# A segment sum and two-layer MLP on one NeuronCore: TensorE's step 0 written out in front of its loop

## The chip, the cores and the metric

The kernel runs on one core of a Trainium2 chip. The metric is the device time of one execution in microseconds (us), the median over several runs. TensorE (PE) does the matmuls, VectorE (DVE), ScalarE (ACT) and GpSimd (POOL) the rest, and SyncE (SP) issues the large DMAs. Each engine works through its own list of instructions, and the engines meet at semaphores.

## The reference

412,500 edges, each with 48 features and a destination node, sorted by destination; 12,500 nodes with 128 features.

```python
h   = maximum(layernorm(x), 0)                     # nodes x 128
agg = segment_sum(edge_attr_48, dst, 12500)        # nodes x 48
u   = graph_globals[0]                             # 64, the same for all nodes
z   = relu(concat([h, agg, u]) @ W1 + b1)          # 240 -> 256
out = x + z @ W2 + b2                              # 256 -> 128
```

## The kernel before

**Tiling.** The edges are cut into groups of 896 (128 partitions with 7 edges each). 19 groups are one step, and there are 25 steps, the last a short one. The nodes are cut into 25 tiles of 512. A step's groups come in five quads: quads 0 to 2 are part 0 (12 groups), quads 3 and 4 are part 1 (7 groups). The edge buffer holds one step; SP loads a quad of the next step when TensorE signals (`edges_used`) that it has used that quad of this one.

**Sums.** For each quad VectorE writes a onehot matrix (`make_onehot`, L795): which of 32 nodes following the group's first an edge belongs to. TensorE multiplies it with the edges into `group_bank` (`sum_quad`, L1043; a 32-column tile for each group). ScalarE copies a part's sums to SBUF (`copy_sums`), VectorE makes the rest of the split (`low_sums`, L831), and TensorE places the part's windows at their nodes with a second onehot matrix, `placing` (`place`, L1065). VectorE adds the placed window to `agg` (`add_window`, L824).

**Positions.** `placing` needs to know where each group stands in its window. GpSimd works that out for all steps at once at the start (`places`, which ends with `spread`, L468). TensorE turns it with five transposes (`turn_places`, L1116) and VectorE copies the result to `const_bank` (L891), after which it can write the first `placing` (L807). VectorE takes its work in the order of the program: behind that copy stand the first `placing`, the moments of the first node tile, more onehots, the `low_sums` of part 1 and the `agg` adds.

**MLP.** `turn_x(k)` (L1082) transposes the normalised node tile k; `first_layer(k)` (L1092, L1096, L1098) and `second_layer(k)` (L1109) run one and two steps after it.

**TensorE's program.** After a few matmuls that keep its clock up (`keep_clock`, L1131) and the transposes of the first destinations (`turn_rel`, L1028), TensorE runs a hardware loop over steps 0 to 23, one body for all of them, with branches for what differs: L1145 (`i > blocks`; `blocks` is 4), L1148 (`i > 1`), L1152 (`i > 0`) and L1159 (`i > 0` around the first layer). In step 0 it takes the branches to `turn_places`, the last block in the chain of Else parts, and past the first layer. In step 1 it takes those to `sum_bias` (L1124). Behind the loop stand the short last step and the end of the MLP.
Of the kernel before, what the change touches and what calls it, by code (L numbers as in the profile page):

```python
# [60 lines left out]
def gnn_kernel(nc, x, dst, edges, graph_globals, w1, b1, w2, b2, out):  # L61
# [8 lines left out]
    full_steps = n_edges // step_edges  # L70
# [22 lines left out]
    with ctx:  # L93
# [6 lines left out]
        def sem(name):  # L100
            return ctx.enter_context(nc.semaphore(name))
# [96 lines left out]
        rel_ready = sem("rel_ready")  # L198
# [57 lines left out]
        def quads_of(s):  # L256
            return LAST_QUADS if s.static and s.value == steps - 1 else QUADS

        def part_quads(s, h):
            if s.static and s.value == steps - 1:  # L260
                return PART_QUADS[0][:len(LAST_QUADS)] if h == 0 else ()
            return PART_QUADS[h]
# [9 lines left out]
        def strips_of(k):  # L272
            return last_width // P if k.value_is_last else NJ
# [6 lines left out]
        def own(k):  # L280
            return 1 if k.static and k.value == tiles - 2 else 0
# [741 lines left out]
        def _(pe):  # L1023
# [9 lines left out]
            def sum_quad(s, q):  # L1033
                g0, ng = quads_of(s)[q]
                h = 0 if q in PART_QUADS[0] else 1
                n = q - PART_QUADS[h][0]
                pe.wait_ge(edges_in[q], s.value * 16 + 16)
                pe.wait_ge(onehot_ready, s.value * NQ + q + 1)
                if n == 0:
                    pe.wait_ge(sums_split[h], s.value + 1)  # L1040
                for r in range(EDGES_PER_ROW):
                    for j in range(ng):
                        done = pe.matmul(  # L1043
                            group_bank[h][WINDOW * j:WINDOW * (j + 1), n * F_EDGE:(n + 1) * F_EDGE],
                            onehot[:, (g0 + j) * EDGES_PER_ROW + r, :],
                            edge_buf[:, g0 + j, r * F_EDGE:(r + 1) * F_EDGE],
                            start=(r == 0), stop=(r == EDGES_PER_ROW - 1))
                done.then_inc(edges_used, 1)

            def sum_part(s, h):  # L1050
                for q in part_quads(s, h):
                    sum_quad(s, q)

            def place(s, h):
                quads = part_quads(s, h)
                pe.wait_ge(sums_split[h], s.value + 2)
                pe.wait_ge(placing_ready[h], s.value + 1)
                if not s.below(1):
                    pe.wait_ge(agg_added, s.value * 2 + h + 2)
                bank = window_bank[h][0:F_EDGE, :].rearrange("f (j i) -> f j i", j=NJ)  # L1060
                for n, q in enumerate(quads):
                    low, high = QUAD_WINDOW[q]
                    rows = quads_of(s)[q][1] * WINDOW
                    for part, sums in enumerate((sums_high, sums_low)):
                        done = pe.matmul(bank[:, :, low // NJ:high // NJ], sums[h][0:rows, n, :],  # L1065
                                         placing[h][0:rows, n, :, 0:(high - low) // NJ],
                                         start=(n + part == 0), stop=(n == len(quads) - 1 and part == 1),
                                         skip_group_check=True)
                done.then_inc(window_ready[h], 1)

            def turn_x(k, to_bank=turned_bank):
                pe.wait_ge(normed, k.value + 1)
                if to_bank is not turned_bank:
                    pe.wait_ge(sums_split[1], full_steps + 1)
                elif isinstance(k, Again):
                    pe.wait_ge(out_copied, k.value + 2)
                else:
                    pe.wait_ge(position_ready, 1)
                    pe.wait_ge(out_copied, k.value + 1)
                pe.wait_ge(turned_copied, k.value + 1)  # L1080
                for j in range(strips_of(k)):
                    done = pe.transpose(to_bank[:, j * P:(j + 1) * P], normed_x[:, j, :], ident[:, :])  # L1082
                done.then_inc(x_turned, 1)

            def first_layer(k):
                pe.wait_ge(w1_split, 1)
                pe.wait_ge(bias_ready, 3)
                pe.wait_ge(turned_copied, k.value + 2)
                cols = strips_of(k) * P
                for c in range(2):  # L1090
                    pe.wait_ge(hidden_copied, k.value * 2 + c + 5)
                    pe.matmul(hidden_bank[c][:, 0:cols], w1_node[:, c * P:(c + 1) * P], normed_t[own(k)][:, 0:cols],  # L1092
                              start=True, stop=False)
                pe.wait_ge(tile_low_ready, k.value + 3)
                for c in range(2):
                    pe.matmul(hidden_bank[c][:, 0:cols], w1_high[:, c * P:(c + 1) * P], tile_sums[own(k)][:, 0:cols],  # L1096
                              start=False, stop=False)
                    pe.matmul(hidden_bank[c][:, 0:cols], w1_low[:, c * P:(c + 1) * P], tile_sums[own(k)][:, 0:cols],  # L1098
                              start=False, stop=True).then_inc(hidden_ready, 1)

            def second_layer(k, to_bank=out_bank):
                pe.wait_ge(hidden_copied, k.value * 2 + 8)
                if to_bank is out_bank:
                    pe.wait_ge(out_copied, k.value + 2)
                    if not isinstance(k, Again):
                        pe.wait_ge(turned_copied, k.plus(2).value + 1)
                for j in range(strips_of(k)):
                    for c in range(2):
                        done = pe.matmul(to_bank[:, j * P:(j + 1) * P], hidden[own(k)][:, c, j * P:(j + 1) * P],  # L1109
                                         w2_sb[:, c, :], start=(c == 0), stop=(c == 1))  # L1110
                done.then_inc(out_ready, 1)

            def turn_places():
                pe.wait_ge(spread_ready, 1)
                for q in range(NQ):
                    done = pe.transpose(out_bank[:, q * steps:(q + 1) * steps],  # L1116
                                        spread[:, q, :, :].rearrange("s j w -> s (j w)"), ident[0:steps, 0:steps])
                done.then_inc(position_turned, 1)

            def sum_bias():  # L1120
                pe.wait_ge(weights_in, 7 * 16)
                pe.wait_ge(rel_ready, 2)
                for c in range(2):
                    done = pe.matmul(hidden_bank[c][:, 0:1], w1_global[:, c * P:(c + 1) * P], global_col[:, :],  # L1124
                                     start=True, stop=True)
                done.then_inc(bias_summed, 1)

            def keep_clock(n, bank):
                ones16 = ones[:, :].bitcast(mybir.dt.bfloat16)
                with pe.Fori(0, n):  # L1130
                    pe.matmul(bank[:, 0:2 * P], ones16[:, 0:P], ones16[:, :], start=True, stop=True)  # L1131
# [7 lines left out]
            keep_clock(8, window_bank[0])  # L1139
            turn_rel(0)  # L1140
            keep_clock(4, window_bank[0])
            with pe.Fori(0, full_steps) as i:
                step = At(0, i)
                sum_part(step, 0)
                with pe.If(i > blocks):  # L1145
                    second_layer(step.plus(-2))
                with pe.Else():
                    with pe.If(i > 1):  # L1148
                        second_layer(step.plus(-2))
                        turn_rel(i - 1)  # L1150
                    with pe.Else():
                        with pe.If(i > 0):  # L1152
                            sum_bias()
                        with pe.Else():
                            turn_places()
                place(step, 0)
                sum_part(step, 1)
                turn_x(step)
                with pe.If(i > 0):  # L1159
                    pe.wait_ge(rel_ready, i * 2)  # L1160
                    first_layer(step.plus(-1))
                place(step, 1)

            final, third, second, last = At(steps - 1), At(tiles - 3), At(tiles - 2), last_tile()
# [63 lines left out]
```

## Time and profile before

| | us |
|---|---|
| median of 3 runs | 270.75 (270.53 to 270.99) |
| the profiled execution | 270.22 |
| its span | 268.1 |
| TensorE busy | 244.8 (91%) |
| VectorE busy | 228.2 (85%) |
| ScalarE / GpSimd busy | 144.3 / 104.2 |
| bytes moved | 94.48 MB, 352 GB/s over the span |
| mean granted TensorE clock | 0.968 of full |

The span is the time between the first and the last instruction of the trace; the profiled execution's time is 2.1 us longer. A granted clock of 1.00 is 2.4 GHz and 0.50 is 1.2 GHz.

### The profile page before, as it was taken

The page shows a single profiled execution, that of the slowest core. Times are in us where ns is not written, and L with a number is a line of the kernel's source. Part 1 is how long each engine was busy: PE and PEld are TensorE (multiplying, and loading weights), DVE is VectorE, ACT ScalarE, POOL GpSimd, SP SyncE. Part 2 cuts the span into 40 slices and gives each one's busy share as a digit, 9 for nine tenths or more (in the row PEclk, how much of TensorE's full clock was granted, in tenths as well). Part 3 has the DMA queues.
Part 4 walks back from the last instruction along what each step waited for, and adds up shares of the span by engine and source line. Part 5 has one row for each costly group of instructions (what it writes and reads, how often), then busy time and mean ns, then how long its engine had stood idle before and what let it go on. Part 6 is the DMA issues. An engine that isn't in the chain of part 4 may idle for free.

```text
span 268.1 us, 17351 instructions
## 1 busy us (share of the span) xinstructions
PE 244.8 (91%) x7438; PEld 199.4 (74%) x7438; DVE 228.2 (85%) x556; ACT 144.3 (54%) x315; POOL 104.2 (39%) x112
## 2 busy tenths in 40 slices
PE   6647699999999999989899989999999989999994
PEld 3546678878878977877787777786797777778753
DVE  1967977898899999988999899999999999897362
ACT  2904447867654755455465366465365545546541
POOL 8761031351453255235135325415424514523410
PEclk9965789999999999999999999999999999999999
DMA  7999989999999999999999999999999999999941
GB/s 246 366 362 349 353 273 333 340 371 328 334 378 380 388 382 381 373 380 381 388 381 382 389 382 382 370 366 374 384 369 367 385 381 383 386 373 317 397 185 55
DMA packets 70873, 94.48 MB, mean 352 GB/s; under 512 B 4324, under 2 KB 64260, under 8 KB 70854
## 3 DMA queue, kind: packets, MB, share of 16 engines
q1 hardware_dynamic: 69802, 94.29, 99.6%
q10 hardware_dynamic: 956, 0.00, 0.2%
q14 instruction: 15, 0.12, 0.1%
q8 instruction: 4, 0.07, 0.1%
q0 software_dynamic: 96, 0.00, 0.0%
HBM read 87.88 MB, written 6.40 MB: 352 GB/s over the span
## 4 chain that ended last, share of the span: by engine, by line
PE 55%; DMA 25%; DVE 12%; issue 5%; DVEq 1%; POOL 1%; ACT 0%; POOLq 0%
DMA edge_buf<-in_edge_attr 23%; PE group_bank L1043 19%; PE out_bank L1109 11%; PE hidden_bank L1092 10%; DVE onehot L795 4%; PE window_bank L1065 4%; PE out_bank L1082 3%; PE hidden_bank L1096 3%; PE hidden_bank L1098 3%; PE hidden_bank L1028 2%; DMA dst_rows<-in_dst 1%; DVE placing L807 1%; DVE bn L840 1%; DVE agg L824 1%; DVE rel_rows L750 1%
## 5 line engine op out<-in xcount | busy, mean ns | idle before, releaser
L795 DVE TENSOR_TENSOR onehot<-rel,const_bank 128x896 f32<-128x896 f32 (+1 forms) x122 | 122.8, 1023 | 8.0 <-issue 7.9
L1043 PE MATMUL group_bank<-edge_buf,onehot 128*32 128x48 f32 x6454 | 89.2, 212 | 5.0 <-DMA edge_buf<-in_edge_attr 3.6
L1043 PEld LDWEIGHTS group_bank<-edge_buf,onehot 128*32 128x32 f32 x6454 | 81.3, 114 | 11.5 <-issue 7.0
L536 POOL TENSOR_TENSOR tile_sums<-agg,tile_sums 48x512 fp32r<-48x512 f32 x23 | 29.2, 1268 | 137.8 <-ACT tile_sums L623 137.8
L1109 PE MATMUL out_bank<-w_sb,hidden 128*128 128x128 f32 x384 | 48.5, 279 | 1.7 <-issue 0.9
L1109 PEld LDWEIGHTS out_bank<-w_sb,hidden 128*128 128x128 f32 x384 | 44.7, 191 | 4.1 <-issue 1.3
L1092 PE MATMUL hidden_bank<-normed_t,w_node 128*128 128x512 f32 (+1 forms) x100 | 46.9, 591 | 0.4 <-ACT hidden L633 0.4
L601 ACT ACTIVATE normed_x<-x_buf,shift,inverse 128x128 f32<-128x128 f32 x98 | 40.3, 492 | 1.3 <-DVE shift L855 1.3
L633 ACT ACTIVATE hidden<-hidden_bank,hidden_bias 128x512 f32<-128x512 f32 (+1 forms) x50 | 31.3, 676 | 11.5 <-PE hidden_bank L1098 11.5
L593 ACT ACTIVATE deviation<-mean_var,eps_col 128x4 f32<-128x4 f32 (+1 forms) x25 | 7.5, 298 | 52.0 <-DVE mean_var L846 52.0
L519 POOL TENSOR_TENSOR xb_buf<-x_buf,b_rows 128x512 f32<-128x512 f32 (+1 forms) x25 | 31.5, 1262 | 7.5 <-DMA x_buf<-in_x 4.2
L531 POOL TENSOR_TENSOR out_buf<-mlp_out,xb_buf 128x512 f32<-128x512 f32 x23 | 29.4, 1277 | 5.6 <-ACT mlp_out L641 3.9
L824 DVE TENSOR_TENSOR agg<-agg,window_bank 48x352 f32 (+1 forms) x49 | 21.6, 441 | 10.7 <-PE window_bank L1065 9.8
L641 ACT ACTIVATE mlp_out<-out_bank 128x512 f32<-128x512 f32 x23 | 13.7, 597 | 29.4 <-PE out_bank L1109 29.4
L1096 PE MATMUL hidden_bank<-tile_sums,w_high 112*128 112x512 f32 (+1 forms) x50 | 29.1, 582 | 0.1
L1065 PE MATMUL window_bank<-placing,sums_high 128*48 128x128 f32 (+3 forms) x122 | 23.1, 247 | 5.6 <-DVE sums_low L831 4.2
L1092 PEld LDWEIGHTS hidden_bank<-normed_t,w_node 128*128 128x128 f32 x100 | 17.3, 194 | 12.8 <-issue 12.6
L807 DVE TENSOR_TENSOR placing<-node_ramp,const_bank 128x456 fp32r<-128x456 f32 (+2 forms) x49 | 24.9, 508 | 0.0
L623 ACT ACTIVATE tile_sums<-agg 48x512 fp32r<-48x512 f32 (+1 forms) x25 | 15.6, 625 | 14.5 <-DVE agg L824 12.1
L1065 PE MATMUL window_bank<-placing,sums_low 128*48 128x128 f32 (+3 forms) x122 | 21.5, 232 | 0.0
L1065 PEld LDWEIGHTS window_bank<-placing,sums_high 128*48 128x48 f32 (+1 forms) x122 | 15.2, 126 | 8.2 <-issue 7.1
L840 DVE BATCH_NORM_STATS2 bn<-x_buf 128x6 f32<-128x128 f32 x98 | 21.0, 271 | 0.0
(97 smaller groups left out, 219.5 us busy)
## 6 DMA issues: line engine op xcount, KB each, us to landing
edge_buf<-in_edge_attr SPq DMA_DIRECT2D x97, 672.0 KB, 7.0
edge_buf<-in_edge_attr SPq DMA_DIRECT2D x24, 504.0 KB, 7.7
x_buf<-in_x SPq DMA_DIRECT2D x24, 256.0 KB, 7.9
out<-out_buf SPq DMA_DIRECT2D x23, 256.0 KB, 5.8
dst_rows<-in_dst SPq DMA_DIRECT2D x3, 448.5 KB, 6.3
dst_rows<-in_dst SPq DMA_DIRECT2D x1, 252.3 KB
out<-out_buf SPq DMA_DIRECT2D x1, 224.0 KB
edge_buf<-in_edge_attr SPq DMA_DIRECT2D x1, 168.0 KB, 5.4
```

Of the source, the lines that this page charges most:

```text
L519: pool.tensor_tensor(xb_buf[k.third][:, 0:nj, :], x_buf[k.parity][:, 0:nj, :], b2_rows[:, :].unsqueeze(1).to_broadcast([P, nj, F_NODE]), A ...
L531: pool.tensor_tensor(out_buf[slot(k)][:, 0:nj, :], mlp_out[:, 0:nj, :], xb_buf[k.third][:, 0:nj, :], ALU.add).then_inc(out_added, 1)
L536: pool.tensor_tensor(sums_tile(k, STACK_LOW), agg_tile(k), sums_tile(k, 0).bitcast(fp32), ALU.subtract)\
L601: done = act.activation(normed_x[:, j, :], x_buf[k.parity][:, j, :], ACT.Relu, bias=shift[:, j:j + 1], scale=inverse[:, j:j + 1])
L633: act.activation(hidden[own(k)][:, c, 0:cols], hidden_bank[c][:, 0:cols], ACT.Relu, bias=hidden_bias[:, c:c + 1]).then_inc(hidden_copied, 1)
L795: dve.tensor_tensor(onehot[:, c0:c0 + cols, :], rel[:, r0:r0 + cols].unsqueeze(2).to_broadcast([P, cols, WINDOW]), ramp_const.unsqueeze(1) ...
L807: dve.tensor_tensor(placing[h][:, 0:nq, :, 0:width], node_ramp[:, :, 0:width].unsqueeze(1).to_broadcast([P, nq, NJ, width]), position_cons ...
L1043: done = pe.matmul(group_bank[h][WINDOW * j:WINDOW * (j + 1), n * F_EDGE:(n + 1) * F_EDGE], onehot[:, (g0 + j) * EDGES_PER_ROW + r, :], ed ...
L1065: done = pe.matmul(bank[:, :, low // NJ:high // NJ], sums[h][0:rows, n, :], placing[h][0:rows, n, :, 0:(high - low) // NJ], start=(n + par ...
L1092: pe.matmul(hidden_bank[c][:, 0:cols], w1_node[:, c * P:(c + 1) * P], normed_t[own(k)][:, 0:cols], start=True, stop=False)
L1096: pe.matmul(hidden_bank[c][:, 0:cols], w1_high[:, c * P:(c + 1) * P], tile_sums[own(k)][:, 0:cols], start=False, stop=False)
L1109: done = pe.matmul(to_bank[:, j * P:(j + 1) * P], hidden[own(k)][:, c, j * P:(j + 1) * P], w2_sb[:, c, :], start=(c == 0), stop=(c == 1))
```

## The change

TensorE's step 0 stands in front of the loop, in the order in which the loop's body did it: the sums of part 0, `turn_places`, the placing of part 0, the sums of part 1, `turn_x`, the placing of part 1. Its waits are on constants. The loop runs from step 1, without the branch of L1152 and without that of L1159. No other engine's program changes. The static program of TensorE becomes longer by one step's instructions and shorter by two branches; the matmuls that run, and their order, stay the same.

```diff
             keep_clock(4, window_bank[0])
-            with pe.Fori(0, full_steps) as i:
+            sum_part(At(0), 0)
+            turn_places()
+            place(At(0), 0)
+            sum_part(At(0), 1)
+            turn_x(At(0))
+            place(At(0), 1)
+            with pe.Fori(1, full_steps) as i:
                 step = At(0, i)
                 sum_part(step, 0)
                 with pe.If(i > blocks):
@@
                         second_layer(step.plus(-2))
                         turn_rel(i - 1)
                     with pe.Else():
-                        with pe.If(i > 0):
-                            sum_bias()
-                        with pe.Else():
-                            turn_places()
+                        sum_bias()
                 place(step, 0)
                 sum_part(step, 1)
                 turn_x(step)
-                with pe.If(i > 0):
-                    pe.wait_ge(rel_ready, i * 2)
-                    first_layer(step.plus(-1))
+                pe.wait_ge(rel_ready, i * 2)
+                first_layer(step.plus(-1))
                 place(step, 1)
```

## Rows read from the trace of the kernel before

**Rows 1.** The page: its header, and the chain's shares by engine

```profile
span 268.1 us, 17351 instructions
...
PE 55%; DMA 25%; DVE 12%; issue 5%; DVEq 1%; POOL 1%; ACT 0%; POOLq 0%
```

**Rows 2.** The chain that ended last, 0 to 45 us: start, us, what

```profile
12.70 1.26 POOL spread L468
13.96 1.86 issue
...
16.59 0.31 DVE const_bank L891
...
30.93 0.23 DVE sums_low L831
```

**Rows 3.** TensorE in order of time: start, us, what [idle before <-releaser]

```profile
9.19 3.21 PE L1043 MATMUL group_bank<-edge_buf,onehot 128*32 128x48 f32 x168 [1.37 <-DVE onehot L795]
15.82 0.72 PE L1116 MATMUL out_bank<-ident,spread 25*128 25x25 f32 x5 [3.42 <-issue]
17.79 0.34 PE L1065 MATMUL window_bank<-placing,sums_high 128*48 128x128 f32 x1 [1.24 <-DVE placing L807]
...
18.66 2.46 PE L1043 MATMUL group_bank<-edge_buf,onehot 128*32 128x48 f32 x98
22.06 1.11 PE L1082 MATMUL out_bank<-ident,normed_x 128*128 128x128 f32 x4 [0.94 <-ACT normed_x L601]
...
24.53 3.59 PE L1043 MATMUL group_bank<-edge_buf,onehot 128*32 128x48 f32 x168
28.29 0.87 PE L1124 MATMUL hidden_bank<-global_col,w_global 64*128 64x1 f32 x4 [0.17 <-issue]
31.29 0.26 PE L1065 MATMUL window_bank<-placing,sums_high 128*48 128x128 f32 x1 [2.12 <-DVE sums_low L831]
```

**Rows 4.** Branch instructions by line: count, ns min/median/max, first and last start

```profile
L1148 PEldq COMPARE_BRANCH  x1: 3099/3099/3099, 12.4 to 12.4; - x1
```

```profile
L1159 PEldq COMPARE_BRANCH  x1: 439/439/439, 22.1 to 22.1; - x1
```

```profile
L1159 PEldq COMPARE_BRANCH  x23: 67/68/83, 33.3 to 248.7; - x23
```

**Rows 5.** DMA queue q8: whole span, then 12.9-13.1, 18.5-18.7, 25.6-25.8 us: packets, MB, share

```profile
q8 instruction: 4, 0.07, 0.1%
```

```profile
q8 instruction: 1, 0.02, 35.6%
```

```profile
q8 instruction: 1, 0.02, 34.5%
```

```profile
q8 instruction: 1, 0.02, 33.0%
```

**Rows 6.** The chain, 30 to 60 us: steps 1, 2 and 3

```profile
33.88 1.05 PE out_bank L1082 x4
...
38.05 0.24 PE window_bank L1065 x4
...
40.53 2.02 PE out_bank L1109 x16
42.55 0.86 PE hidden_bank L1028 x7
...
53.74 0.41 PE window_bank L1065 x6
...
58.71 0.24 PE window_bank L1065 x4
```

**Rows 7.** Stretches: us, busy (count) of PE, PEld, DVE, ACT, POOL, clock, DMA share, GB/s

```profile
29.00:32.40 3.40, 1.28 (x59) 1.09 (x62) 3.40 (x5) 1.29 (x5) 0.00 (x0) 0.99 1.07 389
32.40:35.80 3.40, 3.40 (x70) 2.77 (x59) 3.13 (x12) 0.99 (x3) 2.29 (x2) 0.51 0.83 254
35.80:70.00 34.20, 33.26 (x1017) 27.51 (x1020) 28.28 (x67) 24.59 (x52) 11.76 (x10) 1.00 0.98 339
```

## The prediction

> **What bounds the kernel now.** I read the page first. Its chain lies 55% on TensorE, 25% on DMA and 12% on VectorE [rows 1], an average over stages. So I went to the chain in order of time, and looked at step 0, the one place where the edit takes something away. GpSimd finishes `spread` at 13.96 us. Then the chain shows 1.86 us of "issue", in which nobody is waited for, and only at 15.82 us do the five transposes of L1116 start; VectorE, idle, takes their result at 16.59 us [rows 2]. TensorE itself had been idle for 3.42 us by then [rows 3].
>
> The list of branches names the cause. The branch of L1148, at 12.4 us, lasted 3099 ns; the 23 untaken ones of L1159 took 67 to 83 ns [rows 4]. The instruction queue shows a 16 KB packet within 12.9 to 13.1 us [rows 5]: the branch went to code that was not there yet, and it was released at 12.4 + 3.1 = 15.5 us. Two more packets come near 18.6 and 25.7 us, and of the four of the whole span that leaves one for the 240 us that follow [rows 5]. So once fetched the loop stays in, and each piece of code is fetched once.
>
> From 16.6 to 31.2 us the chain runs down VectorE's list (the `low_sums` of step 1, at 30.93 us, release the placing at 31.29 us, for which TensorE had idled 2.12 us) [rows 2, 3]. From there TensorE is continuously busy at 35.8 to 70 us (33.26 of 34.20 us) while DMA is not full (0.98 and 339 GB/s) [rows 7]. A DMA there starts when TensorE has used a quad, so whatever step 1 ends early or late is handed on to the end, one for one.
>
> **The change, part by part: what it takes away.** In the new order the transposes need no branch. They wait for `spread` alone and start at about 14.0 us: 15.82 - 13.98 = 1.84 us sooner. All that hangs on them moves along: placing at 15.95 (17.79), the sums of part 1 at 16.8 (18.66), `turn_x` at 20.2 (22.06), part 0 of step 1 from 22.7 to 26.3 (24.53 to 28.12), `low_sums` done at 29.3 (31.16) [rows 2, 3]. If nothing else moved, the kernel would gain 1.84 us.
>
> The branch of L1159 costs 68 ns in each of 23 passes [rows 4], 1.6 us if it were exposed. It is hidden: the sequencer executes it at 33.3 us, when the transposes before it only start at 33.88 us [rows 4, 6]. I take 0, with 1.6 us as the upper bound of the gain. The branch of L1152 runs in steps 0 and 1 alone.
>
> **What it adds: code that is read for the first time.** Before, step 1 ran through code that step 0 had already brought in. Now it runs through a second copy, and that has to be fetched. Where are the borders of the pieces? Count a pair as two instructions. One border lies between the branch of L1148 (which waited for a piece) and its target, that is behind 336 instructions of part 0, 32 of the second layer, 46 of the second layer and `turn_rel` of the next block [rows 3, 6] and some 10 waits. The next lies at the branch of L1159, whose one execution of 439 ns stands out [rows 4]: 8 + 10 + 12 + 196 + 8 instructions and 10 to 20 waits further. A piece is about 250 instructions, so the border ahead of these is about 175 instructions into part 0, passed at roughly 10.5 us.
>
> Now the fetch. The piece entered at 10.5 us was followed by a packet at 13.0, the one entered at 15.5 by one at 18.6, the one entered at 22.5 by one at 25.7: each time the next piece is asked for when a piece is entered, and its packet comes 2.5 to 3.2 us later. From the packet to the release was 15.5 - 13.0 = 2.5 us. So a piece is there 5.0 to 5.7 us after the piece before it was entered; as low as 4.7 if the first was entered at 10.8. I take 5.2, nearest the one case that shows both ends.
>
> In the new order the borders fall as follows. *C*: 161 left in part 0, then 22 + some waits, so 60 into part 1 of step 0, reached at 17.4 us; it is in since 15.5. *D*: 95 instructions into part 0 of step 1, reached at 23.7; asked for at 17.4, in at 22.6. No stall, with 1.1 us to spare. *E*: asked for at 23.7, in at 28.9. Its border is just behind part 0 of step 1, ahead of the target of L1145's branch, reached at 26.3: **a stall of 2.6 us**. It delays `sum_bias` (0.87 us [rows 3]) to 29.1 to 30.0 us, and so the placing to 30.0 us, where VectorE is ready at 29.4. Against 31.29 that is still 1.3 us ahead. *F*: asked for at 28.9, in at 34.1. Its border is some 150 instructions into the 196 of part 1 of step 1, which starts at 30.6: reached at 32.1, **a second stall of 2.0 us**. The last 46 instructions take 0.5 us, so part 1 is done at 34.6 instead of 33.88 [rows 6]: 0.7 us later than before. With 4.7 us a piece it is done at 33.6 (-0.3), with 5.8 at 35.8 (+1.9).
>
> **The clock.** In rows 7 the granted clock is 0.99 (the 2.4 GHz level) in 29.0 to 32.4 us, 0.51 (1.2 GHz) in 32.4 to 35.8, behind TensorE's idle 2.12 us, and 1.00 after. What that costs: from the placing at 31.29 to that at 38.05 step 1 takes 6.76 us, step 3 takes 58.71 - 53.74 = 4.97 [rows 3, 6]; of the 1.79 us I put 0.2 to the cold start of the placing, which leaves 1.6 us for 3.4 us of low clock, 0.47 for each. Before, the low stretch left 2.4 us behind the point that *F*'s border marks (33.4 us): 1.1 us lost. In the new order TensorE idles again ahead of 34.1 us; if it then needs as long to get the clock back as after its restart at 31.29 (4.5 us, 3.4 to 4.5 of them low), it loses 1.6 to 2.1 us. The difference is +0.5 to +1.0; I take +0.8, with 0 and +1.3 as bounds.
>
> **The sum.** -1.84 (branch stall), +2.5 (the two piece stalls, net of what VectorE would have made TensorE wait in any case: the end of part 1 goes from 33.88 - 1.84 = 32.0 to 34.6 us, together +0.7), + 0.8 (clock) + 0 (L1159) = +1.5 us. On the profiled execution's own 270.22 that is 271.7; the median of the runs shown is 0.5 us above it, so 270.75 + 1.5 = 272.3 us. The bounds of the parts give -0.3 to +3.2.
>
> **Rivals.** (1) *The fetch keeps ahead in straight code, and the edit does what it says: 1.84 us gained, 268.9 us.* For it: no row shows a stall in straight code; the 3.1 us stood at a taken branch. Against it: in the trace the sequencer entered pieces only 5 us or more apart, so nothing tested it, and all three packets came 2.5 us or more after the entry. It decides if a piece arrives within some 2.5 us of the request (*E* at 26.3). The Trainium skill, in "Runtime: NRT & Kernel Launch", section "Instruction fetch mechanics", says that the sequencer fetches the next 16 KB block while it executes the current one, that crossing is mostly hidden, and that a taken branch out of the window stalls; by that rule this rival would be the outcome, and the trace so far agrees only on the branch. (2) *Only one stall shows, or they give back just the gain*: pieces of 4.7 us and no clock loss end near 270.5, an early *F* near 269.9. The same place, another price. (3) *The loop no longer fits*: its 690 or so instructions lie across four pieces before and after, so I expect no refetch; if each pass fetched one piece and waited only 1 us, it would be some 294 us. (4) *The branch of L1159 was exposed after all*: 1.6 us more gained.
>
> **How the numbers follow.** Two piece stalls with or without the clock: 0.56, 271.3 to 274.2 us. Cancelling (2): 0.17, within 0.2% (0.54 us, about what a measurement of this kernel tells from no change) of 270.75. Rival 1 with the better half of 2: 0.25; with 4: 0.01. Rival 3: 0.01. That is 0.26 faster, 0.17 same, 0.57 slower. The likeliest case's own range is 271.0 to 274.0; the range that holds 8 in 10 has to reach over rival 1: 268.8 to 274.0.
>
> **What would show it.** Right, step by step: L1116 starts at 14.0 us with no 3 us branch; q8 packets near 20, 26.5 and 31.5 us, and another behind; L1145's first branch lasts 2 to 3 us at 26.3; a gap inside the second quad of part 1 of step 1, near 32 us; the granted clock low until 38 us or so. Wrong: `turn_x` in step 1 starting near 32 us, with more q8 packets ahead of need, gives rival 1; q8 packets in every pass give rival 3.

## The result and the profile after

The changed kernel takes 273.11 us (median of 20 runs, 270.88 to 275.06) where the kernel before takes 270.97 (20 runs, 270.08 to 272.33). The ratio is 1.0068, with a 95% interval of 1.0048 to 1.0089: 0.7% slower. Medians here are of all executions; the ratios leave out those that took over 1.5% more than the fastest of their kernel. The execution profiled is the longest of the 20, 275.06 us, so the sizes of its stalls are read beside a second profile of the same kernel (e1_again, 272.05 us).

The chain of work of the changed kernel in step 1 (start, us, what):

```profile
23.97 3.26 PE group_bank L1043 x168
27.23 3.52 issue
...
32.61 1.91 PE group_bank L1043 x78
34.51 1.59 issue
36.10 0.80 PE group_bank L1043 x20
```

The transposes in order of time on TensorE, and VectorE's wait behind them:

```profile
14.01 0.49 PE L1116 MATMUL out_bank<-ident,spread 25*128 25x25 f32 x5 [0.99 <-POOL spread L468]
```

```profile
17.03 0.68 DVE L840 BATCH_NORM_STATS2 bn<-x_buf 128x6 f32<-128x128 f32 x3 [1.53 <-DMA x_buf<-in_x]
```

The branch of `i > blocks` (L1151 in the changed file; the branch of L1145 in the kernel before), by line, and the instruction queue on the page and in 27.8 to 27.9 us:

```profile
L1151 PEldq COMPARE_BRANCH  x1: 3362/3362/3362, 26.9 to 26.9; - x1
```

```profile
q8 instruction: 7, 0.11, 0.2%
```

```profile
q8 instruction: 1, 0.02, 62.2%
```

Two things are to be seen. The stall of step 0 is gone: the transposes start at 14.01 us instead of 15.82 [rows 3], and their releaser is now `spread`. And step 1 has two stalls of "issue" that it didn't have: 3.52 us at the branch, and 1.59 us in the middle of matmuls that no branch stands between, behind 78 of 98 pairs. Seven pieces of code are fetched instead of four [rows 5]. In steps 0 and 1 five packets come, at 13.8, 20.0, 27.9, 33.7 and 40.1 us, where before three came, at 13.0, 18.6 and 25.7; the others come behind 260 us.

The granted clock (stretches; columns as in [rows 7]):

```profile
26.80:30.30 3.50, 0.43 (x36) 0.29 (x27) 3.44 (x8) 1.83 (x5) 0.00 (x0) 0.99 1.05 391
30.30:36.20 5.90, 3.86 (x93) 3.50 (x96) 3.56 (x6) 1.04 (x3) 2.01 (x2) 0.50 0.87 282
36.20:40.40 4.20, 4.20 (x29) 2.53 (x28) 2.52 (x12) 0.55 (x2) 0.51 (x1) 0.50 0.94 316
40.40:70.00 29.60, 28.59 (x930) 24.61 (x929) 23.88 (x51) 22.68 (x47) 7.76 (x7) 1.00 0.90 307
```

It is at the 1.2 GHz level for 10 us, from 30.3 to 40.4, where before the stretch of step 1 at that level was 3.4 us long [rows 7]. Ahead of it both kernels have it low as well (0.50 in 15.3 to 28.9 us before, and in 16.6 to 26.8 us now).

The placing of part 0 (the first L1065 of a step) is a good clock for the program. Its start in each step, from the timelines, in us:

| kernel | step 0 | 1 | 2 | 5 | 9 | 23 |
|---|---|---|---|---|---|---|
| before | 17.79 | 31.29 | 43.17 | 73.02 | 110.23 | 246.85 |
| changed | -2.15 | +0.38 | +3.91 | +3.98 | +4.35 | +4.74 |
| e1_again | -1.91 | -0.78 | +2.22 | +2.24 | +3.46 | +1.85 |
| e1_branch_back | -2.16 | -0.68 | +2.68 | +2.75 | +4.48 | +3.42 |
| e1_places_first | -1.82 | -1.81 | -0.56 | +0.27 | +1.13 | +2.72 |
| e1_two_steps | -1.92 | -1.89 | +2.88 | +2.72 | +3.41 | +4.58 |
| e2_before_fill | +0.67 | +0.67 | +1.19 | +1.23 | +1.77 | +1.22 |
| e2_after_fill | -0.11 | +1.74 | +3.13 | +3.20 | +4.10 | +2.82 |
| e2_one_test | -2.07 | -2.07 | -2.29 | -2.40 | -0.85 | -1.45 |
| e2_one_test_busy | -1.13 | -1.82 | -3.53 | -3.48 | -2.63 | -3.45 |
| e3_before_busy | +0.04 | +0.04 | +0.03 | +0.06 | +0.98 | +1.11 |

The row "before" has the times, the others the differences from it. All that the edit wins and loses happens ahead of step 2. Up to step 5 the difference stands still, and it is still there, give or take a microsecond, at step 23. One profile of each kernel stands behind a row; the times of the kernels below are medians of several runs.

### The profile page after: what moved, and what is told of

It reads as the page before. It is cut to its first block, busy times and chain, and to the rows that moved or that the text cites. A ratio compares the mean times of both kernels' runs of the same rounds, so it can differ in the third digit from the quotient of the medians.

```text
span 272.8 us, 17314 instructions
## 1 busy us (share of the span) xinstructions
PE 246.3 (90%) x7438; PEld 200.0 (73%) x7438; DVE 228.6 (84%) x556; ACT 144.6 (53%) x315; POOL 104.2 (38%) x112
## 4 chain that ended last, share of the span: by engine, by line
PE 52%; DMA 30%; DVE 7%; issue 6%; SPq 2%; DVEq 1%; ACT 0%
DMA edge_buf<-in_edge_attr 26%; PE group_bank L1043 19%; PE out_bank L1109 10%; PE hidden_bank L1092 9%; PE window_bank L1065 4%; DMA x_buf<-in_x 4%; PE out_bank L1082 3%; PE hidden_bank L1096 2%; PE hidden_bank L1098 2%; SPq L343 2%; DVE onehot L795 2%; PE hidden_bank L1028 1%; DVE bn L840 1%; DVE agg L824 1%; DVE rel_rows L750 1%
## 5 line engine op out<-in xcount | busy, mean ns | idle before, releaser
L1092 PE MATMUL hidden_bank<-normed_t,w_node 128*128 128x512 f32 (+1 forms) x100 | 47.7, 601 | 0.4 <-ACT hidden L633 0.4
L531 POOL TENSOR_TENSOR out_buf<-mlp_out,xb_buf 128x512 f32<-128x512 f32 x23 | 29.4, 1277 | 5.6 <-ACT mlp_out L641 3.9
L1092 PEld LDWEIGHTS hidden_bank<-normed_t,w_node 128*128 128x128 f32 x100 | 17.5, 196 | 13.1 <-issue 12.8
L1065 PE MATMUL window_bank<-placing,sums_high 128*48 128x128 f32 (+3 forms) x122 | 23.1, 247 | 3.2 <-DVE sums_low L831 1.9
L1065 PE MATMUL window_bank<-placing,sums_low 128*48 128x128 f32 (+3 forms) x122 | 21.5, 232 | 0.0
L1082 PE MATMUL out_bank<-ident,normed_x 128*128 128x128 f32 x96 | 16.6, 299 | 3.3 <-ACT normed_x L601 3.3
```

What stands on the lines that cost most here:

```text
L531: pool.tensor_tensor(out_buf[slot(k)][:, 0:nj, :], mlp_out[:, 0:nj, :], xb_buf[k.third][:, 0:nj, :], ALU.add).then_inc(out_added, 1)
```

## The experiments

**The change once more.** No edit.

> The changed kernel once more, for a second profile. Piece theory (each 16 KB piece of TensorE's code is asked for on entering the one before and is there 5 to 6 us later): two stalls at the same instructions as in the first profile, the branch of L1145 in step 1 for 2 to 3.5 us and a gap of 1 to 2.5 us behind about 78 pairs of part 1 of step 1; 0.3 to 1.1% slower than before. Rival (the stalls were a disturbance of one execution): they are at other places or absent, and the time is within 0.2% of before or below it.

Measured: 272.11 us, ratio 1.0032 (1.0001 to 1.0064). By line, the branch; and part 1 of step 1 on TensorE:

```profile
L1151 PEldq COMPARE_BRANCH  x1: 3922/3922/3922, 25.2 to 25.2; - x1
```

```profile
34.94 0.80 PE L1043 MATMUL group_bank<-edge_buf,onehot 128*32 128x48 f32 x20 [1.59 <-issue]
```

The same two places, to the instruction: again 20 pairs are left. The branch took longer than the 3.5 us expected at most. The stalls belong to the program.

**The branches in another order, no second copy.**

```diff
 # the kernel before
                 sum_part(step, 0)
-                with pe.If(i > blocks):
+                with pe.If(i < 1):
+                    turn_places()
+                with pe.Else():
+                    with pe.If(i > blocks):
...
```

> The kernel before with the branches in another order: turn_places is the first block behind part 0 (if i < 1), inside the piece already fetched, and there is no second copy of a step. Piece theory: no 3 us branch, transposes at 14.0 to 14.3 us, no stall in step 1, 1.2 to 1.9 us faster than before (0.4 to 0.7%). Rival (what helps or hurts is the branch itself, or the transposes were not what step 1 waits for): within 0.2% of before.

Measured: 272.06 us, ratio 1.0027 (0.9996 to 1.0057): no gain, where 1.2 to 1.9 us were expected. The first half came as told: step 1's placing is 1.81 us early. But by step 2's placing the lead is 0.56 us, and from there it melts by 0.28 us a step up to step 5. The first loss goes with the clock: from the first to the second placing of step 1 it takes 7.76 us (before, 6.76), with the clock low for 6.8 us (28.4 to 35.2) instead of 3.4. The rest is in the chain of every step. The stretch, and the chain in step 2:

```profile
28.50:35.10 6.60, 5.63 (x110) 4.55 (x111) 5.62 (x16) 1.18 (x3) 2.53 (x2) 0.50 1.02 344
```

```profile
39.39 0.58 issue
39.98 2.02 PE out_bank L1109 x16
```

One more branch now stands ahead of the second layer: TensorE is idle there for 0.58 us in steps 2 to 4 (before, 0.32 for two branches) and for 0.32 in most later steps (before, 0.04 for one). Behind 168 short matmuls the sequencer seems to have no lead left, so a branch there is paid for in every step.

**Step 1 written out as well.**

```diff
 # the changed kernel
             place(At(0), 1)
-            with pe.Fori(1, full_steps) as i:
+            sum_part(At(1), 0)
+            sum_bias()
+            place(At(1), 0)
+            sum_part(At(1), 1)
+            turn_x(At(1))
+            pe.wait_ge(rel_ready, 2)
+            first_layer(At(0))
+            place(At(1), 1)
+            with pe.Fori(2, full_steps) as i:
...
```

> The changed kernel with step 1 written out too, so that step 1 has no branch at all and the loop starts at step 2. Piece theory: step 1 stalls in straight code (a gap of 1 to 3 us within its instructions) and step 2, the loop's first pass, is new code again, some three pieces of 5.5 us each for a step of 10.3 us: 4 to 7 us slower than the changed kernel, 278 to 280 us. Rival (only taken branches into new code stall, straight code is fetched ahead): step 1 has no stall, and the time is 269 to 272 us.

Measured: 272.98 us, ratio 1.0055 (1.0016 to 1.0093). Both theories missed. Step 1 has no stall of code; I read that as its pieces lasting longer without the blocks that step 1 jumps over, and VectorE releases its placing in any case. The stall comes in the loop's first pass, in straight code, with the clock low again behind it (41.1 to 44.5 us):

```profile
36.91 1.64 PE L1043 MATMUL group_bank<-edge_buf,onehot 128*32 128x48 f32 x133
41.42 1.01 PE L1043 MATMUL group_bank<-edge_buf,onehot 128*32 128x48 f32 x35 [2.87 <-issue]
```

I had multiplied pieces by 5.5 us, and left out the waits behind which a fetch can be hidden. "Only taken branches stall" falls too.

**The removed branch back.** `with pe.If(i > 0):` around `first_layer`, in the changed kernel.

> The changed kernel with the branch around the first layer kept in the loop (if i > 0, always true there). If the branch is hidden as I took it: within 0.2% of the changed kernel. If its 68 ns were exposed: 1.6 us slower than the changed kernel.

Measured: 273.22 us, ratio 1.0054 (1.0022 to 1.0085), and the changed kernel measured beside it 1.0032 (1.0001 to 1.0064). The intervals overlap and leave the question to the profiles: from step 2 to step 5 it takes 29.92 us, the changed kernel in its two profiles 29.92 and 29.87. The branch costs nothing there.

**The borders moved.** The same 110 instructions, once in each kernel:

```diff
             keep_clock(4, window_bank[0])
+            ones16 = ones[:, :].bitcast(mybir.dt.bfloat16)
+            for _ in range(55):
+                pe.matmul(window_bank[0][0:WINDOW, 0:16], ones16[:, 0:WINDOW], ones16[:, 0:16],
+                          start=True, stop=True)
```

> The kernel before with 55 tiny matmuls (110 instructions, 32 weights by 16 columns, results unused) in TensorE's idle time ahead of part 0 of step 0. They change no other work and shift every border of a piece 110 instructions forward. Piece theory: the border that lay at L1148's branch now lies in the third quad of part 0 of step 0, about 80 of 112 instructions in: a gap of 2 to 4 us in the middle of straight matmuls there, no 3 us at the branch of L1148 any more, transposes at 15 to 16 us; time within 0.4% of before. Rival (the 3 us are the taken branch's own): L1148's branch still lasts 3 us, no gap in part 0.

> The changed kernel with the same 110 instructions. Piece theory: a gap of 2 to 4 us in the third quad of part 0 of step 0, which costs 1 to 1.7 of the 1.8 us won; the stall at L1145's branch in step 1 goes down from 3.4 to 3.9 us to under 1.5 us, because its piece is asked for 3 us sooner, and the gap behind 78 pairs of part 1 moves forward to about 20 pairs and is under 2 us. Part 1 of step 1 ends at 33.5 to 34.5 us instead of 36.9 and 35.7: 1 to 2.5 us faster than the changed kernel, within 0.4% of before. Rival (the length of the code, not the place of the borders): same or slower than the changed kernel.

The kernel before with them: 271.65 us, ratio 1.0027 (1.0000 to 1.0054). TensorE in step 0, and the branch of `i > 1` by line:

```profile
11.18 0.65 PE L1043 MATMUL group_bank<-edge_buf,onehot 128*32 128x48 f32 x41 [0.29 <-DMA edge_buf<-in_edge_attr]
15.47 0.37 PE L1043 MATMUL group_bank<-edge_buf,onehot 128*32 128x48 f32 x15 [3.64 <-issue]
```

```profile
L1151 PEldq COMPARE_BRANCH  x1: 223/223/223, 15.9 to 15.9; - x1
```

This is the clearest of the runs. The stall has left the branch, which takes 223 ns now, and stands behind the 41st of 56 pairs of the third quad; 40 had been worked out. The transposes start at 16.49 us, a little behind the 15 to 16 expected. The 3 us were never the branch's.

The changed kernel with them: 274.19 us, ratio 1.0158 (1.0113 to 1.0203), where 1 to 2.5 us less than the changed kernel had been expected. The gap in part 0 came where it should (3.47 us), but a piece that I had in time by 1 us was late:

```profile
24.16 0.27 PE L1082 MATMUL out_bank<-ident,normed_x 128*128 128x128 f32 x1 [1.56 <-issue]
...
30.87 1.19 PE L1043 MATMUL group_bank<-edge_buf,onehot 128*32 128x48 f32 x48 [4.09 <-issue]
```

The place of each stall is foretold by the borders; the size is not, as the time from the entry to the packet went from 1.3 to 6.3 us here. The time itself decides nothing: the rival by length was told as "same or slower", and slower it is, by 0.9%. What speaks for the borders is where the gaps stand, each some 250 instructions behind the last, those jumped over counted.

**The loads made light.** In both kernels, for `s.value > 0` only the first group of each quad is loaded (`ng = 1`), so that the later steps sum stale edges.

> The kernel before with light loads: from step 1 on each quad's DMA brings only its first group (a quarter to a third of the bytes), so the sums of the later steps are over stale edges. It is the partner of e3_after_light. TensorE then bounds all steps at 9.2 us and DMA is never full: 260 to 263 us. The code pieces' packets wait behind less data: from entering a piece to its packet under 2 us wherever step 0's loads are done (from some 16 us on); the 3 us at L1148's branch in step 0 stay, as step 0's loads are the full ones.

> The changed kernel with the same light loads (later steps sum stale edges). If the time to fetch a piece is mostly its wait behind the edge loads: packets within 2 us of the entry, the stall at L1145's branch in step 1 down from 3.4 to 3.9 us to under 1.5 us, the gap in part 1 under 0.5 us, and the kernel 0.5 to 2 us faster than e3_before_light. Rival (a fixed time for each piece, or the new code costs by its length): stalls as before, 3 to 4 us and 1.6 us, and 1 to 3 us slower than e3_before_light.

Measured: 267.07 us (ratio to the full kernel before 0.9851, 0.9813 to 0.9889) and 266.17 (0.9810, 0.9772 to 0.9847); the first was expected at 260 to 263, and why it isn't faster is left open. With DMA light the change comes out 0.9 us ahead by the medians of four executions each; the intervals overlap, and the two profiled executions are level (266.76 and 266.70). The branch in step 1 of the changed kernel, by line, and TensorE there:

```profile
L1153 PEldq COMPARE_BRANCH  x1: 1642/1642/1642, 25.8 to 25.8; - x1
```

```profile
30.97 2.46 PE L1045 MATMUL group_bank<-edge_buf,onehot 128*32 128x48 f32 x98
```

Its packets come at 25.1 and 28.5 us, the second 1.1 us after the branch was released into the piece ahead of it (27.5 us); in the full kernel that took 3.5 us (30.2 to 33.7). The branch is a little over the 1.5 us expected; part 1 runs through in one go, as told. So of the 5.9 us of a fetch there with full loads, 2.4 are a wait that goes when the edges' loads go.

The pair also has the clock's price, with little DMA beside it. At step 1's placing the changed kernel is 1.16 us ahead, at step 2's 0.13: between them it takes 12.72 us with the clock low for 6.8 us (28.7 to 35.5), its partner 11.69 us with 3.4 (31.1 to 34.5).

**One branch ahead of the second layer.**

```diff
 # the kernel before; replaces L1145 to L1155
+                with pe.If(i > 1):
+                    second_layer(step.plus(-2))
+                    with pe.If(i < blocks + 1):
+                        turn_rel(i - 1)
+                with pe.Else():
+                    with pe.If(i < 1):
+                        turn_places()
+                    with pe.Else():
+                        sum_bias()
```

> One loop over all steps as before, with the branches in another order: if i > 1: second layer, and behind it if i < blocks + 1: turn_rel; else if i < 1: turn_places, else sum_bias. One branch stands ahead of the second layer instead of one or two, and turn_places lies in a piece that is there. Piece theory plus the price of 0.27 us that a branch ahead of the second layer showed in e1_places_first: step 1's placing 1.7 us sooner than before, steps 2 to 4 0.27 us shorter each, no loss in steps 5 to 9: 1.5 to 2.5 us faster than before (268.5 to 269.5), if the clock does not take it back. Rival (what is won early is lost by the end, as DMA bounds the rest): within 0.2% of before.

Measured: 268.80 us, ratio 0.9916 (0.9884 to 0.9947). Transposes at 13.99 us, step 1 2.07 us early, no stall of code. The issue ahead of the second layer in steps 2 to 4 is 0.04 to 0.05 us, but those steps are only 0.1 us shorter and not 0.27 (10.23 us for step 2, before 10.33): `turn_rel`, now behind the second branch, takes 1.02 us instead of 0.86. Of the 2.40 us of step 5, part is given back by step 9. There the chain lies on the edge DMA from 69.07 us on (9.03 us), in the kernel before only from 108.36.

**The clock.** In the block of step 1, alone and with the order above:

```diff
                         sum_bias()
+                        pe.wait_ge(agg_added, 4)
+                        ones16 = ones[:, :].bitcast(mybir.dt.bfloat16)
+                        for _ in range(10):
+                            pe.matmul(window_bank[0][:, 0:2 * P], ones16[:, 0:P], ones16[:, :],
+                                      start=True, stop=True)
```

> The same with ten matmuls of 256 columns in bf16 behind sum_bias in step 1 (results unused, 1.1 us at the high clock), while TensorE waits for VectorE. If the low clock in steps 1 and 2 costs what I took (0.47 us for each us): the low stretch behind the restart is gone in most executions, 0.5 to 1.5 us faster than e2_one_test. Rival (the clock falls anyway or is high anyway there): the same as e2_one_test within 0.2%.

> The kernel before with ten matmuls of 256 columns in bf16 behind sum_bias in step 1 (results unused) and nothing else: the clock part alone. If the low clock behind TensorE's 2.1 us of idle time costs what e2_one_test against e2_one_test_busy showed: 1 to 2 us faster than before, the 3 us at L1148's branch unchanged. Rival (the gain of e2_one_test_busy over e2_one_test was luck in the place of the clock's changes): within 0.2% of before.

Measured: 266.97 us, ratio 0.9862 (0.9832 to 0.9893), and in the kernel before alone 268.93 us, 0.9923 (0.9892 to 0.9954). The ten matmuls wait for step 0's `agg` adds, which read the bank that they write. The stretch behind TensorE's idle time, in e2_one_test_busy and in the profile of e3_before_busy:

```profile
28.60:32.40 3.80, 2.94 (x110) 2.54 (x111) 3.80 (x8) 0.86 (x2) 0.79 (x1) 1.00 1.06 379
```

```profile
32.20:35.40 3.20, 3.20 (x91) 2.92 (x80) 2.97 (x8) 0.88 (x2) 1.85 (x2) 0.50 0.66 200
```

In the first the clock stays high, and the way from step 1's placing to step 2's takes 10.18 us. In the profile of e2_one_test, with the clock low from 29.4 to 32.8 us, that takes 11.67: 1.5 us for 3.4 us of low clock. In the second profile the clock fell all the same, and the same way takes 11.88 us, as in the kernel before. That execution took 271.37 us, the longest of the seven of its kernel (268.46 the shortest), but what it lost against the kernel before it lost behind step 5, not here.

So that the matmuls work by the clock is shown in one pair of profiles, for e2_one_test_busy. For the 0.8% of e3_before_busy it is not: no faster execution of it was profiled, and the mean granted clocks of its executions (0.965 to 0.984) are no higher than those of the kernel before beside it (0.959 to 0.985). The rival, that the added code moves something else, was not tried. In e2_one_test_busy it does: two branches of step 0 (L1150, L1161) take 2.3 and 1.9 us, where none is over 0.3 in e2_one_test, and step 0's placing is 0.9 us later. e2_one_test_busy, 1.4% below the kernel before, is still the version that beats both.

## Why the prediction was right

**What it removes.** Right: the start of the transposes was told as 14.0 us and is 14.01, the branch of 3 us is gone. One cover was not priced: in the first profile VectorE then waited 1.53 us for the first node tile's DMA, until 17.03 us, so step 1's part 0 starts at 23.9 us instead of 22.7. Up to that point only 0.6 of the 1.84 us were left in that execution; in e1_again the part starts at 22.5.

**What it adds.** Right in mechanism and place. The borders were told as the target of the first branch of step 1, and 150 instructions into part 1; they are that target, and 156. The stalls are 3.5 to 4.1 and 1.6 us instead of 2.6 and 2.0. The term that was too small is the 5.2 us for a piece. In the changed kernel the piece entered at 30.2 us was followed by a packet at 33.7 and that one's code ran at 36.1: 5.9 us, just above the highest that I had counted with (5.8). From packet to code it is 2.2 to 2.6 us at every stall of every run; what varies is the wait ahead of the packet. A smaller term was left out: from the branch's release at 30.2 us to the first matmul behind it at 30.75 another 0.5 us pass. Part 1 of step 1 ends at 36.9 and 35.7 us where I had 34.6: +3.0 and +1.9 us against the kernel before, where the sum has +0.7 with +1.9 as its bound.

**The clock.** The direction was right: low for 10.2 us in both profiles of the kernel, against 3.4. From the end of part 1 to step 2's placing it took back 0.9 us in the one and 0.4 in the other (3.91 - 3.02, 2.22 - 1.86), for the 0.8 taken. What low clock costs was taken as 0.47 us for each us; the pair e2_one_test and e2_one_test_busy gives 1.5 us for 3.4, or 0.44, and the pair with light loads 1.0 us for 3.4 more, or 0.30.

**The branch of L1159.** 0 was right (e1_branch_back).

**Handed on to the end.** Mostly right for time lost: from +3.9 and +2.2 us at step 2 to +4.7 and +1.9 at step 23. For time won it is not one for one: e2_one_test has 2.40 us at step 5 and 1.45 at step 23. The sum was +1.5 us, and the medians give +2.1 (20 runs) and +1.1 (12 runs). The way and the places were right, but that the total is so near owes something to luck: the two profiled executions are 4.8 and 1.8 us above the profiled one of the kernel before, and the stalls in them cost more than the sum has.

**The rivals.** The fetch that keeps ahead is out, by stalls in straight code in five kernels (the changed one, e1_two_steps, e1_branch_back and the two with 110 instructions more). By the rule that I quoted from the Trainium skill, "Runtime: NRT & Kernel Launch", section "Instruction fetch mechanics", crossing a block is mostly hidden; the traces disagree where code is read for the first time with DMA full (stalls of 1.6 to 4.1 us at crossings), and agree that the next block is fetched while the current one runs (the packet of 33.7 us comes while the piece entered at 30.2 runs). The loop still fits: no packet comes in its later passes.

What stays open: how long a request waits ahead of its packet couldn't be foretold (1.3 to 6.3 us), and why e2_after_fill met the longest of these waits was not tried. Open too is why the ten matmuls make e3_before_busy faster.

## What to carry to other kernels

Writing a loop's first pass out buys the jump but doubles the code that is read cold, and cold code comes in pieces that wait behind the kernel's own loads. Where one branch stalls, look first whether its target can be moved forward, into a piece that is there; but count the branches that this puts behind a run of short matmuls, as each is paid in every pass. Where TensorE waits a few microseconds for another engine and the clock falls behind the wait, try giving it something to do, and read the clock in the profile afterwards.

## What the runs showed of the hardware

- Straight code stalls at the border of a 16 KB piece: 3.64 us in the kernel before with 110 instructions put in front, with no branch near. With light loads the changed kernel had one stall, of 1.6 us, instead of two.
- From an instruction packet to the first instruction of its piece, 2.2 to 2.6 us at all stalls; from the entry of a piece, where a stall marks it, to the packet of the next, 0.8 and 1.1 us with light loads and 1.3 to 6.3 us with full ones.
- A branch behind 168 short matmuls costs 0.27 us of TensorE's time (0.58 us of issue for three, 0.32 for two, 0.04 for one); one behind four transposes none.
- TensorE was idle for 2.1 us in step 1 of the kernel before, and the granted clock was 0.51 in the next 3.4 us [rows 3, 7]. With ten unused matmuls, 1.27 us, in such an idle stretch it stayed at 1.00 in one kernel's profile (e2_one_test_busy) and fell in the other's (e3_before_busy). In two pairs of profiles, 3.4 us more of low clock went with 1.0 and 1.5 us more of time.
